# Window attention on one core: score transpositions in pairs over two PSUM banks, and a new order of the groups

## The reference

```python
qkv = xw @ qkv_w + qkv_b                       # windows of 8x8 tokens, 4 heads of 16
scores = einsum('bhqd,bhkd->bhqk', q, k) / (|q| |k|) / tau
scores = scores + bias + mask
attn = softmax(scores, axis=-1)                # over the 64 keys of a window
out = einsum('bhqk,bhkd->bhqd', attn, v) @ proj_w + proj_b
skip = x + layer_norm(out)
```

## Time and profile before

| | us |
|---|---|
| Median of 3 runs | 782.54 |
| Lowest and highest run | 778.04, 782.89 |
| Span of the profiled execution, first to last instruction | 778.6 |
| PE busy in it | 665.7 (86%) |
| DVE, ACT, POOL busy | 516.4, 480.4, 355.1 |

### The profile page before, as it was taken

How to read it: one execution, slowest core, us unless ns; L and a number is a source line. 1 busy time by engine, 2 the same in 40 slices (tenths; PEclk the granted TensorE clock), 3 DMA queues, 4 the chain that set the end, 5 groups by cost and what they waited for, 6 DMA issues and landing times. The chain is left out here.

```text
span 778.6 us, 21192 instructions
## 1 busy us (share of the span) xinstructions
PE 665.7 (86%) x8584; PEld 371.4 (48%) x8584; DVE 516.4 (66%) x997; ACT 480.4 (62%) x963; POOL 355.1 (46%) x441
## 2 busy tenths in 40 slices
PE   4785789999999999999998579999999988749880
PEld 2562455565565555655555232233333367735350
DVE  4796487877777787877778322577777786372181
ACT  3565266777777777777775548877777656624000
POOL 4696446778777777788776520022221123100000
PEclk9787599999999999999999959999999999969955
DMA  9550000000000000000000020122112220120278
GB/s 216 137 128 11 1 3 2 3 2 3 2 3 3 3 3 3 3 2 3 3 2 3 2 56 1 28 55 56 33 50 55 55 55 2 31 72 2 63 194 269
DMA packets 15719, 31.44 MB, mean 40 GB/s; under 512 B 7488, under 2 KB 9284, under 8 KB 15620
## 3 DMA queue, kind: packets, MB, share of 16 engines
q1 hardware_dynamic: 12592, 29.16, 14.1%
q10 hardware_dynamic: 2760, 0.66, 0.5%
q0 software_dynamic: 272, 0.27, 0.2%
HBM read 20.71 MB, written 9.37 MB: 39 GB/s over the span
## 5 line engine op out<-in xcount | busy, mean ns | idle before, releaser
L794 POOL TENSOR_TENSOR sc<-sc,mx 128x512 f32<-128x512 f32 x128 | 133.7, 1044 | 102.4 <-DVE mx L725 102.4
L722 DVE TENSOR_TENSOR sc<-s_ps,bias_tab 128x512 f32<-128x512 f32 x128 | 87.7, 685 | 52.6 <-PE s_ps L528 52.6
L1424 POOL TENSOR_TENSOR square<-xs 128x1024 f32<-128x1024 f32 x16 | 34.1, 2133 | 165.5 <-DVE xs L1166 165.5
L539 PE MATMUL t_ps<-consts,sc 128*128 128x128 f32 x512 | 84.4, 288 | 16.2 <-ACT pt L656 12.5
L656 ACT ACTIVATE pt<-t_ps 128x512 f32<-128x512 f32 x128 | 75.7, 592 | 31.2 <-PE t_ps L539 30.1
L539 PEld LDWEIGHTS t_ps<-consts,sc 128*128 128x128 f32 x512 | 54.3, 142 | 84.8 <-issue 48.1
L725 DVE TENSOR_REDUCE mx<-sc 128x8 f32<-128x512 f32 x128 | 87.8, 686 | 4.4
L1081 ACT ACTIVATE hs<-h_ps,fb1s 128x512 f32<-128x512 f32 x128 | 78.2, 689 | 19.1 <-PE h_ps L990 19.0
L528 PE MATMUL s_ps<-kx,qu 32*64 32x128 f32 x2048 | 72.3, 278 | 3.5 <-DVE kx L749 2.9
L990 PE MATMUL h_ps<-xs,fw 64*128 64x512 f32 x256 | 68.7, 650 | 1.0 <-ACT hs L1081 1.0
L528 PEld LDWEIGHTS s_ps<-kx,qu 32*64 32x64 f32 x2048 | 56.7, 134 | 15.2 <-issue 13.4
(11 more groups left out here) (207 smaller groups left out, 1295.2 us busy)
## 6 DMA issues: line engine op xcount, KB each, us to landing
raw<-in_x_dram SPq DMA_DIRECT2D x32, 256.0 KB, 5.1
xr<-in_x_dram SPq DMA_DIRECT2D x32, 256.0 KB, 3.9
out_dram<-x SPq DMA_DIRECT2D x32, 256.0 KB, 3.9
rec_scratch<-r SPq DMA_DIRECT2D x4, 224.0 KB, 2.5
w<-in_L_conv_W_dram SPq DMA_DIRECT2D x1, 784.0 KB
w<-in_L_conv_W_dram SPq DMA_DIRECT2D x1, 672.0 KB
xs<-rec_scratch SPq DMA_DIRECT2D x16, 28.0 KB
xs<-rec_scratch ACTq DMA_DIRECT2D x16, 28.0 KB
```

The lines of the kernel that those rows point to most:

```text
L539: last = pe.transpose(t_ps[:, m], sc[n % KEPT][:, m].rearrange("c h k -> c (h k)"), ident)
L722: dve.tensor_tensor(sc[n % KEPT][:, :, :, :], s_ps[j][:, :, :, :], bias_tab[:, j, hp], ALU.add)\
L794: pool.tensor_tensor(v, v, mx[n % KEPT][:, :].unsqueeze(2).broadcast_to([128, 8, TOK]), ALU.subtract)\
```

## The change

- `t_ps` becomes two banks, and the former bank `n_ps` is its second half: norms and variances now go through bank 1 of `t_ps`.
- `turn(p, k)` does a pair of blocks, 2k into bank 0 and 2k+1 into bank 1, and signals once. Its first half waits for the exponential of the pair before; its second half waits besides until ACT has read norms and variances out of bank 1. In turn `norms` and `variances` wait for the exponential of the turn ahead of them.
- `exponent(p, k)` is one instruction of 1024 columns over both banks; there are 4 for each pair of images in place of 8.
- `KEPT` is 8, so DVE may fill eight score tiles before it has to wait for a turn.
- The lists of PE and ACT are in a new order. Those of DVE and POOL are as before.

```diff
-            KEPT = 4
+            KEPT = 8
...
-            t_ps = ps(stage, "t_ps", [128, 4, 128])
+            t_ps = ps(stage, "t_ps", [128, 2, 4, 128])
-            n_ps = ps(stage, "n_ps", [128, COLS])
+            n_ps = t_ps[:, 1].rearrange("c m k -> c (m k)")
...
             def norms(pe, p):
-                    after(pe, s["norm_ln"], p)
+                    after(pe, s["exped"], turns_before(p + 1, "norms"))
...
+            def turn(pe, p, k):
+                if there(p, PAIRS):
+                    for i in range(2):
+                        n = 8 * p + 2 * k + i
+                        pe.wait_ge(s["shifted"], n + 1)
+                        if i == 0:
+                            after(pe, s["exped"], 4 * p + k)
+                        else:
+                            after(pe, s["norm_ln"], p + 1 + (k >= TURNS_BEFORE["norms"]), PAIRS)
+                            after(pe, s["var_ln"], p - 1, PAIRS)
+                        for m in range(4):
+                            last = pe.transpose(t_ps[:, i, m], sc[n % KEPT][:, m].rearrange("c h k -> c (h k)"), ident)
                     last.then_inc(s["turned"], 1)
...
+            def exponent(act, p, k):
+                    act.wait_ge(s["turned"], 4 * p + k + 1)
                     after(act, s["mixed"], 2 * (p - 1) + a + 1)
+                    act.activation(pt[a][:, 2 * hp:2 * hp + 2].rearrange("c b m k -> c (b m k)"),
+                                   t_ps[:, :, :, :].rearrange("c b m k -> c (b m k)"), ACT.Exp).then_inc(s["exped"], 1)
...
             def tensor_step(pe, n):
-                turn(pe, n - 2, 0)
                 score(pe, n - 2, 1)
...
```

More of the change, by code:

```diff
@@ L429, in build @@
             kx = [[sb(stage, f"kx{k}{a}", [128, 2, COLS]) for a in range(2)] for k in range(2)]
-            pt = [[sb(stage, f"pt{a}{b}", [128, 4, 128]) for b in range(4)] for a in range(2)]
+            pt = [sb(stage, f"pt{a}", [128, 4, 4, 128]) for a in range(2)]
             sc = [sb(stage, f"sc{k}", [128, 4, 2, TOK]) for k in range(KEPT)]
@@ L530, in score, with turns_before @@
                     last.then_inc(s["scores"], 1)
-            def turn(pe, p, b):
+            def turns_before(n, what):
+                return min(4 * PAIRS, max(0, 4 * (n - 2)) + TURNS_BEFORE[what] * (0 <= n - 2))
+            def turn(pe, p, k):
                 if there(p, PAIRS):
[L535 to L539, removed]
+                    for i in range(2):
[8 more added lines that the diff above has]
+                            last = pe.transpose(t_ps[:, i, m], sc[n % KEPT][:, m].rearrange("c h k -> c (h k)"), ident)
                     last.then_inc(s["turned"], 1)
@@ L544, in mix @@
                 if there(p, PAIRS):
-                    pe.wait_ge(s["exped"], 8 * p + 4 * a + 4)
+                    pe.wait_ge(s["exped"], 4 * p + 2 * a + 2)
                     if a == 0:
@@ L557, in mix @@
                                 pe.matmul(b_ps[0][rows(2 * j + hp), TOK * at:TOK * (at + 1)], vd[p % 2][:, WIN * j + at, a, hp],
-                                          pt[a][2 * hp + j][:, 2 * i + m, TOK * w:TOK * (w + 1)], start=True, stop=True)
+                                          pt[a][:, 2 * hp + j, 2 * i + m, TOK * w:TOK * (w + 1)], start=True, stop=True)
                     for j in range(2):
                         for hp in range(2):
-                            last = pe.matmul(b_ps[1][rows(2 * j + hp), :], ones, pt[a][2 * hp + j][:, :, :],
+                            last = pe.matmul(b_ps[1][rows(2 * j + hp), :], ones, pt[a][:, 2 * hp + j],
                                              start=True, stop=True)
@@ L581, in variances @@
                     pe.wait_ge(s["csq"], 2 * p + 2)
[L582 to L585, removed]
+                    after(pe, s["exped"], turns_before(p + 4, "variances"))
+                    after(pe, s["norm_ln"], p + 3, PAIRS)
+                    after(pe, s["var_ln"], p)
                     for g in range(4):
@@ L648, in spread_values @@
                     last.then_inc(s["v_out"], 1)
-            def exponent(act, p, b):
+            def exponent(act, p, k):
                 if there(p, PAIRS):
-                    a, hp, j = b // 4, b // 2 % 2, b % 2
-                    act.wait_ge(s["turned"], 8 * p + b + 1)
+                    a, hp = k // 2, k % 2
+                    act.wait_ge(s["turned"], 4 * p + k + 1)
                     after(act, s["mixed"], 2 * (p - 1) + a + 1)
-                    act.activation(pt[a][2 * hp + j][:, :, :], t_ps[:, :, :], ACT.Exp).then_inc(s["exped"], 1)
+                    act.activation(pt[a][:, 2 * hp:2 * hp + 2].rearrange("c b m k -> c (b m k)"),
+                                   t_ps[:, :, :, :].rearrange("c b m k -> c (b m k)"), ACT.Exp).then_inc(s["exped"], 1)
             def sum_recip(act, p, a):
@@ L720, in bias_max @@
                     dve.wait_ge(s["scores"], n // 2 + 1)
-                    after(dve, s["turned"], n - KEPT + 1)
+                    after(dve, s["turned"], (n - KEPT) // 2 + 1)
                     dve.tensor_tensor(sc[n % KEPT][:, :, :, :], s_ps[j][:, :, :, :], bias_tab[:, j, hp], ALU.add)\
@@ L803, in build @@
             STEPS = range(PAIRS + 5)
+            TURNS_BEFORE = {"variances": 0, "norms": 1}
             def tensor_step(pe, n):
-                turn(pe, n - 2, 0)
                 score(pe, n - 2, 1)
@@ L809, in tensor_step @@
                 project_queries(pe, n - 1)
-                turn(pe, n - 2, 1)
+                turn(pe, n - 2, 0)
                 values(pe, n - 1)
                 score(pe, n - 2, 2)
-                turn(pe, n - 2, 2)
                 norms(pe, n - 1)
                 spread_rstd(pe, n - 4)
-                turn(pe, n - 2, 3)
+                turn(pe, n - 2, 1)
                 score(pe, n - 2, 3)
-                turn(pe, n - 2, 4)
                 spread_first(pe, n - 1)
-                turn(pe, n - 2, 5)
-                turn(pe, n - 2, 6)
+                turn(pe, n - 2, 2)
                 mix(pe, n - 2, 0)
-                turn(pe, n - 2, 7)
                 score(pe, n - 1, 0)
                 project_heads(pe, n - 3)
+                turn(pe, n - 2, 3)
                 mix(pe, n - 2, 1)
@@ L857, in scalar_step @@
                 copy_queries(act, n - 2, 1)
+                exponent(act, n - 3, 0)
                 spread_values(act, n - 2, 0)
-                exponent(act, n - 3, 2)
                 spread_values(act, n - 2, 1)
                 norm_log(act, n - 2)
-                exponent(act, n - 3, 3)
                 norm_exp(act, n - 2)
-                exponent(act, n - 3, 4)
-                exponent(act, n - 3, 5)
+                exponent(act, n - 3, 1)
                 by_rows(act, n - 5, 0)
@@ L868, in scalar_step @@
                     by_rows(act, n - 5, 1)
-                exponent(act, n - 3, 6)
+                exponent(act, n - 3, 2)
                 sum_recip(act, n - 3, 0)
-                exponent(act, n - 3, 7)
+                exponent(act, n - 3, 3)
                 if n - 4 != LAST:
@@ L877, in scalar_step @@
                 copy_keys(act, n - 1, 1)
-                exponent(act, n - 2, 0)
                 var_log(act, n - 4)
@@ L881, in scalar_step @@
                 copy_queries(act, n - 1, 0)
-                exponent(act, n - 2, 1)
             def pool_step(pool, n):
```

## The result

The changed kernel takes 812.74 us (median of 4 runs, 811.71 to 813.77) against 781.85 us for the kernel before (4 runs): 1.0398 times as long, 95% interval 1.0371 to 1.0425, so 31 us slower. The forecast was 819, with a range of 806 to 830. The profiled execution has a span of 810.3 us, 31.7 more than before.

What follows compares the result with a forecast made beforehand. PE was taken as the bound in the attention; five new waits, 3.32 us less 0.78, gave +2.54 us a step, +38 us over 15 steps: 817 or 821 by starting point, taken as 819, range 806 to 830.

Steps and rivals of the forecast that it cites:

- the old one: PE's transpositions waiting for ACT's exponential between two back-to-back turns, 0.78 us a step, 15 times; forecast to end.
- A: PE's wait at the second half of turn 1 for ACT's norm_log to read bank 1: 0.44 us a step.
- C: PE's wait ahead of the next score, for DVE's first two of four scale_keys: 0.63 us a step.
- D: PE's wait ahead of project_heads, for all four of DVE's scale_keys: 0.32 us a step.
- E: PE's wait ahead of the second mix, for ACT's exponential of turn 3: 1.30 us a step.
- B: PE's wait ahead of the first mix, for DVE's two scale_queries: 0.63 us a step.
- I keep 21.25 us of PE work for a step: PE's own work in each attention step was taken as unchanged at 21.25 us, as no matmul is added or removed.
- What I costed at nothing: Waits of norms, turn 2 and turn 3 for exponentials 0, 1 and 2, claimed covered by other PE work: 0 us.
- the bounds given for it: Margins on the time: exponential -7 to +2 us, DVE-to-PE step -1 to +2, earlier norm_log -7, run spread 4.5 below to 0.4 above.
- DVE was not in time: Rival, 8%: PE's waits for DVE stay hidden, giving 797 us, or 790 without the norm_log wait too.
- No wait was given back: Rival, 4%: matmuls behind the new waits run shorter, weights loaded while PE waits; 771 us if all 3.32 return.
- The clock stayed at 0.99: Rival, 5%: waits make PE's clock fall to 1.2 GHz at times; two such steps cost 36 us more, 855.

Runs made afterwards that it cites:

- the last run: Changed kernel with turn 3 before score, exponential 2 between the by_rows, score 3 before turn 1, spread_rstd before norms: 771.42 us, 0.9857 of the kernel before.

## Why the prediction was right, and where its size was off

- **The mechanism** was right: PE bound, in order, five waits at the five named places, the old one gone, and nothing else in a middle step. A, C, D and E were each removed by an edit that covers that wait; B was only brought down, from 0.73 to 0.33.
- **The waits**, counted from start to start as the prediction did: A 268.22 - 267.27 - 0.59 = 0.36 (0.44 forecast). A pair of turns has a pitch of 1.03 (below), so B = 272.70 - 270.88 - 1.03 = 0.79 (0.63), C = 275.29 - 272.70 - 1.96 = 0.63 (0.63), D = 276.65 - 275.29 - 1.03 = 0.33 (0.32), E = 279.88 - 277.67 - 1.03 = 1.18 (1.30). Sum 3.29, forecast 3.32. That the sums agree so closely is luck in part: B is 0.16 longer, and A and E are 0.08 and 0.12 shorter.
- **The term that was mis-sized** is "I keep 21.25 us of PE work for a step": it measured 24.03 - 3.29 = 20.74, which the prediction had named as a sign of being wrong. Eight transpositions in a row take 1.02 to 1.05 us from start to start (250.96 to 251.98 and 235.16 to 236.21 in the last run), where two runs of four take 2 x 0.59 = 1.18. The pair ahead of `values` takes 0.93 (261.37 to 262.30); before, a single turn of 0.49 stood there (row below, with 247.60 in the earlier trace rows) and another of 0.59 elsewhere, so 0.15 less as well. Three of the four pairs stay whole in the changed kernel (A splits turn 1): 0.45 us a step. In the last run all four are whole: 21.25 - 0.60 = 20.65. The rows of the kernel before did not show it: the only two turns in a row there have the 0.78 us wait between them.

```profile
247.11 0.66 PE L539 MATMUL t_ps<-consts,sc 128*128 128x128 f32 x4
```

- **Where the step is shorter than forecast**: turn 0 gives 0.15. From turn 3 to the second mix it is 2.21 (277.67 to 279.88) against 1.18 + 1.30 = 2.48: 0.15 by the pair, the rest by ACT's release and the exponential. From `values` to the second half of turn 1 it is 5.92 (262.30 to 268.22) against 6.00. The 0.15 of turn 2 is not gained: DVE sets when the first mix may start, 3.92 us behind score 3 (268.78 to 272.70; forecast 3.91), so B grew by what the pair saved. Together that is 0.5 us a step, 15 steps, 7 to 8 us, which is what lies between the forecast +38 and the measured +31.
- **The assumed values**: DVE releases PE after 0.14 to 0.15 us (275.15 to 275.29; 276.50 to 276.65), as taken. For ACT 0.14 was too much here: 0.09 at A (268.13 to 268.22) and 0.06 at E (279.82 to 279.88). The exponential of 1024 columns takes 1.02 us, near the Square of the earlier trace rows.
- **What I costed at nothing** stayed at nothing: no wait for exponentials 0 and 1 in a middle step, and none for exponential 2 as long as turn 3 stood late: it ends at 275.39, and turn 3 starts at 277.67. The early turn 3 gave this cover up and paid 0.88 us.
- **The range**: the bounds given for it add up to 800 to 823 around 819, so 806 to 830 was a judgement and no sum; 812.74 lies in both.
- **The rivals**: DVE was not in time. No wait was given back: `project_heads` behind D takes 1.02 up to the next work (276.65 to 277.67), as before (262.00 to 263.02), and the four transpositions behind A take 0.56 (268.22 to 268.78), as those behind the old wait did. The clock stayed at 0.99.

## What to carry to other kernels

In an engine that works through a fixed list, merging two small steps into one wide one moves the place where the result is needed nearer to the place where it is made; count the work that stands between each producer and its consumer before and after; where that engine is the bound, each shortfall is added in full, once a step. Work saved directly ahead of such a wait is not gained, as at turn 2. A merge can save work and still lose: the same pairs stand in an order that is 10 us faster than the kernel before and in one that is 31 us slower. When a wait appears, look first for one line to move under it, and check what the moved line itself waits for on the other engines.

## What the runs showed of the hardware

Float32 transpositions of 128x128 in longer runs take less time each: four take 0.59 us up to the next work and eight 1.02 to 1.05, so the second four add 0.43 to 0.46. Ahead of `values` four take 0.49 in the kernel before and eight 0.93. ACT begins on a result of PE 0.04 us after the end that the profile gives it (278.76 to 278.80), while PE begins on a result of ACT or DVE 0.06 to 0.15 us after its end (279.82 to 279.88, 276.50 to 276.65).
